# A fused adaLN and FFN kernel on one core: the conv's products moved in TensorE's row order, and the order of VectorE's and ScalarE's work around them

## The reference

```
h   = gelu(gelu(cond @ W0 + b0) @ W1 + b1);  att = softmax(h @ W2 + b2)
y   = einsum('boi,bih->boh', einsum('bk,koi->boi', att, weight), x) + (att @ bias_k)[:, :, None]
x   = x + y @ (A @ B.T).T + bias                       # rank 128
c   = conv1d(x, w, 9 taps, pad 4, 4 groups of 16 channels) + (cond @ cw.T + fside)[:, :, None]
g   = one_hot(argmax(c @ gate.T + expert_bias))        # 4 experts
out = x + c @ W_up + sum_e g_e * (c @ loraA_e.T) @ loraB_e.T
```

## Time and profile before

| | us |
|---|---|
| median of 3 executions | 1209.54 (1209.33 to 1210.42) |
| profiled execution | 1208.7 |
| its span | 1207.0 |
| TensorE busy | 1162.7 (96%) |
| weight loads busy | 1051.9 |
| VectorE busy | 751.2 (62%) |
| ScalarE busy | 503.1 (42%) |

### The profile page before, as it was taken

The page is one execution under the profiler, slowest core; times in us unless marked ns, Lnnn a source line. Parts: engine busy times, 40 slices in busy tenths (PEclk is TensorE's granted clock), DMA queues, the critical chain, the costliest instruction groups (busy, mean ns, idle before and its releaser), DMA issues.

```text
span 1207.0 us, 19065 instructions
## 1 busy us (share of the span) xinstructions
PE 1162.7 (96%) x7404; PEld 1051.9 (87%) x7404; DVE 751.2 (62%) x1440; ACT 503.1 (42%) x1048; POOL 4.0 (0%) x17
## 2 busy tenths in 40 slices
PE   6598999999999999999999999999999999999998
PEld 5487889889988989988989998988998898998898
DVE  6755766566666556666556666656666656666642
ACT  6544444334344334344334444433444433434320
POOL 1000000000000000000000000000000000000000
PEclk9699999999999999999999999999999999999999
DMA  9744545445544554544544544445544454454211
GB/s 339 240 92 94 141 104 140 113 138 136 118 102 129 132 126 131 141 97 115 143 113 132 140 110 105 137 112 139 137 112 106 130 129 128 132 126 109 56 50 53
DMA packets 115742, 151.78 MB, mean 126 GB/s; under 512 B 21324, under 2 KB 93516, under 8 KB 111404
## 3 DMA queue, kind: packets, MB, share of 16 engines
q1 hardware_dynamic: 115044, 148.36, 47.3%
q10 hardware_dynamic: 608, 2.20, 0.5%
HBM read 80.87 MB, written 35.68 MB: 97 GB/s over the span
## 4 chain that ended last, share of the span: by engine, by line
PE 88%; ACT 6%; DVE 3%; issue 2%; DMA 1%; SPq 0%; ACTq 0%
PE O L864 55%; PE F L847 9%; PE F L811 7%; ACT F L382 5%; PE F L835 4%; PE F L781 3%; PE F L782 3%; PE F L783 3%; PE O L882 2%; PE O L875 1%; PE F L798 1%; PE F L799 1%; SPq L228 0%; DMA xTr<-in_xT_dram 0%; DVE wks L642 0%
## 5 line engine op out<-in xcount | busy, mean ns | idle before, releaser
L864 PE MATMUL O<-Wh,yh 128*128 128x292 f32 (+2 forms) x1536 | 509.0, 331 | 3.2 <-DVE yl L576 3.2
L864 PE MATMUL O<-Wl,yh 128*128 128x292 f32 (+2 forms) x1536 | 498.6, 325 | 0.0
L864 PE MATMUL O<-Wh,yl 128*128 128x292 f32 (+2 forms) x1536 | 498.3, 324 | 0.0
L864 PEld LDWEIGHTS O<-Wh,yh 128*128 128x128 f32 x1536 | 290.6, 189 | 28.6 <-DVE yl L576 3.5
L864 PEld LDWEIGHTS O<-Wh,yl 128*128 128x128 f32 x1536 | 290.0, 189 | 22.5
L864 PEld LDWEIGHTS O<-Wl,yh 128*128 128x128 f32 x1536 | 290.8, 189 | 17.1
L382 ACT ACTIVATE F<-F,cbX 128x128 f32<-128x128 f32 x496 | 138.1, 341 | 219.0 <-PE F L835 218.9
L609 DVE TENSOR_TENSOR osb<-O,x 128x256 f32<-128x256 f32 (+1 forms) x192 | 97.7, 509 | 108.1 <-PE O L882 107.8
L568 DVE STREAM_TRANSPOSE yr<-F 128x512 f32<-128x512 f32 x128 | 91.4, 715 | 83.4 <-PE F L847 83.4
L309 ACT ACTIVATE u<-F 128x256 f32<-128x256 f32 x64 | 24.6, 385 | 263.4 <-PE F L783 219.0
L542 DVE TENSOR_TENSOR x<-F,x 128x512 f32<-128x512 f32 x128 | 87.6, 689 | 32.3 <-PE F L811 32.3
(11 more groups left out here) (126 smaller groups left out, 1470.3 us busy)
## 6 DMA issues: line engine op xcount, KB each, us to landing
x<-in_xP_dram SPq DMA_DIRECT2D x64, 516.0 KB, 4.4
Xr<-x SPq DMA_DIRECT2D x512, 64.5 KB, 2.5
xTr<-in_xT_dram SPq DMA_DIRECT2D x32, 1024.0 KB, 5.1
out_dram<-osb SPq DMA_DIRECT2D x64, 512.0 KB, 2.9
agb<-agb_scratch SPq DMA_DIRECT2D x31, 128.0 KB, 3.3
Wr<-in_Wd_dram SPq DMA_DIRECT2D x2, 1024.0 KB, 15.1
agg_scratch<-stage ACTq DMA_DIRECT2D x1, 2048.0 KB, 11.3
agg<-agg_scratch SPq DMA_DIRECT2D x60, 32.0 KB, 2.3
```

Source lines behind the costliest of these rows:

```text
L864: last = pe.matmul(O[c][:, 0:w_], w[:, t % YR, k, :], m[:, k, c0:c0 + w_], start=k == 0 and n_ == 0, stop=k == 7 and n_ == 2)
```

## The change

Three things are reordered; no instruction is added, removed or resized. On TensorE the shared products and their users stand at other rows. In VectorE's loop, one transposition of the conv and the expert chain of the second tile change places with their neighbours. In ScalarE's loop, zst of the second tile is copied ahead of the high parts of the next conv input. In the setup, ScalarE copies the first shared products ahead of vh of set 1 and of part 4 of the weights, and VectorE's list follows.

```diff
@@ scalar, setup
             xs(0, 0)
-            vhi(1)
-            w(4)
             pc(0, 0)
             pc(0, 1)
             xs(0, 1)
             ys(0, 0)
+            vhi(1)
+            w(4)
             w(5)
@@ scalar, loop, it > 0
                     pc(it + 1, 2)
                     ys(it + 1, 0)
                     pc(it + 1, 3)
+                    zt(2 * it + 1)
                     xs(it + 2, 0)
                     ys(it + 1, 1)
-                    zt(2 * it + 1)
                     bias(it + 3)
@@ vector, setup
             vv(1)
-            vlo(1)
             xd(0, 1)
             ty(0, 0)
             ty(0, 1)
-            w(4)
             ys(0, 0)
             xs(0, 1)
+            vlo(1)
+            w(4)
@@ vector, loop, it > 0
                     ty(it + 1, 0)
-                    ty(it + 1, 1)
                     txl(it + 3, 1)
                     f(t, 2)
+                    ty(it + 1, 1)
                     xd(it + 2, 0)
                     ys(it + 1, 0)
                     ty(it + 1, 2)
+                    zc(t + 1)
                     ty(it + 1, 3)
-                    zc(t + 1)
                     xs(it + 2, 0)
                     ys(it + 1, 1)
                     f(t + 1, 0)
@@ tensor, loop
-                    pp, cc = ((24, 27, 39, 42), (26, 29, 41, 44)) if it == 0 else ((16, 19, 22, 26), (19, 22, 26, 30))
+                    pp, cc = ((24, 28, 39, 42), (28, 32, 42, 45)) if it == 0 else ((16, 21, 26, 31), (21, 26, 31, 34))
                     if n in cc:
                         unit_c(it + 1, cc.index(n))
                     if n in pp:
```

## The result

The changed kernel takes 1190.76 us (median of 4, 1189.13 to 1191.15) against 1209.56 before (median of 4, 1209.33 to 1210.42): ratio 0.9841, 95% interval 0.9824 to 0.9858, or 18.8 us faster. The prediction was 1184.9 with a range of 1181 to 1192. The time lies in the range near its upper end, with 5.9 us less gain than forecast. The profiled execution took 1190.71, its span 1189.0.

What follows compares the result with a forecast made beforehand. TensorE's work (busy 96%) plus the places where it stands was taken to bound the kernel. 23.8 - 1.5 + 1.0 + 0.2 + 1.1 = 24.6 us off gave 1184.1 profiled, 1184.9 as median; range 1181 to 1192.

Steps and rivals of the forecast that it cites:

- part 1: Loop: shared products and users five rows apart remove two waits of 0.41 in each of 29 passes, 23.8 us off.
- wait at the pass's start: First weight load waits for VectorE's residual addition: 0.05 a pass, 1.5 us back; rival of 0.2 to 0.8, chance 0.18.
- The expert chain: VectorE, second tile: moved chain ends 1.6 ahead of TensorE's turn, costing nothing; behind the fourth transposition it would hold TensorE 1.1.
- SP's queue: Loop: raw-set loads issue 5.4 later, the next expert chain slips 0.4, its transposition has 2.1 of slack; no cost.
- the slower rival: Loop: late raw sets, with loads issuing slower, hold VectorE at Xd ahead of the expert chain; about 1228, chance 0.04.
- Pass 0: Later users lengthen the wait for expert values at row 36 to about 3.3; pass 0 together 0.2 us off.
- the case that I gave 0.22: Rival: the longer gap ahead of row 36 of pass 0 drops the clock, 1.7 more, 1186.6 us; chance 0.22.
- Setup: ScalarE's copies first: first users go at 48.3 instead of 49.28, row 0 at 54.4; 1.0 us off.
- Pass 1: Rows 20 and 21 (0.71) run inside the wait for ScalarE's copies, a second wait (0.41) goes: 1.1 us off.
- the fall of the clock near 108: Pass 0: clock drop behind the 2.63 gap costs 1.7 us; might vanish with the gap's new start, taken at nothing.

Runs made afterwards that it cites:

- a3: The changed kernel with ScalarE's loop order of before, zst of the second tile again behind the high parts of the next conv input: 1184.3 us.
- b2: The changed kernel with the first residual addition of the second tile ahead of yl in VectorE's loop: 1190.1 us.
- a4: The changed kernel with the rows of pass 0 put back to those of before: 1188.4 us.
- d1: The changed kernel with ScalarE's loop order and the rows of pass 0 both those of before: 1185.0 us.
- b1: The changed kernel with VectorE's expert chain of the first tile ahead of Xd of the last set in pass 30: 1190.1 us.
- c1: The changed kernel with zst back, the expert chain first in pass 0, and the expert chain ahead of Xd in pass 30: 1184.6 us.
- d2: Against d1, shared products and users in the loop four rows apart instead of five: 1187.2 us.
- b4: The changed kernel with VectorE's expert chain of the second tile back behind the fourth transposition: 1229.1 us.
- b3: The changed kernel with the expert chain behind VectorE's first transposition in pass 0 and zst copied ahead of Xh there: 1191.2 us.

## Why the prediction was right and where it was short

The time lies in the range, and its main term, part 1, is right in mechanism and size. But that the range holds it is partly luck: its upper part, up to 1192, was there for a wait at the pass's start of 0.3 in each pass, and that wait came out at 0.1. What filled it were the end, which the forecast had at nothing, and the clock in pass 0.

- **Part 1, right.** Both waits of each pass are gone, 58 in all; a pass without any other wait takes 35.02 (a3) where it was 35.84: 0.82, as worked out. That a wait of 0.35 costs 0.41 is confirmed by it. The spare of 0.4 was there (0.44).
- **The expert chain, right, a little off in size.** It ends 1.2 ahead of the transposition (forecast 1.6), and behind the fourth transposition it would cost 1.28 (forecast 1.1).
- **The new wait at the pass's start, right, undersized:** 0.10 against 0.05; a3 and b2 both remove it. The term that was too small is the way from VectorE's addition to TensorE's load, 0.12 and not 0.05; the chain up to the addition's end came out as worked out, 5.65 behind the load of the transposition (forecast 5.63).
- **SP's queue: the step that failed.** "So this costs nothing" had 2.1 of slack at the transposition, less the 0.4 by which the chain slips. That holds in passes with layer-0 work: 1.5 to 1.6 is left in most passes whose loads take 5.05, and there Xd was 7.07 behind the first of the eight loads, as forecast. It doesn't hold in pass 30, where TensorE comes to the transposition 3.5 sooner: 2.7 us at the end, of which a3 gives back all. And once the eight loads took 6.57, 0.4 us. The mechanism was in the text as the slower rival, priced with the slack of a full pass for all passes; I had not asked which pass has the least. The rival's "in the loop they take 5.0 to 5.1 throughout" was wrong too. The trace of before already has 12 of 56 sets of eight loads between 135 and 1135 us above 5.3, among them this one:

```profile
176.59 6.37 SPq L228 DMA_DIRECT2D Xr<-x  x8
```

- **Pass 0, the wait right, its price wrong.** The wait for the expert values grew to 3.7 at the loads (3.3 at the matmul), as forecast. The clock then fell, which I had taken at nothing with a bound of 1.7:

```profile
92.00:94.00 2.00, 0.00 (x0) 0.00 (x0) 1.76 (x10) 1.61 (x2) 0.00 (x0) 0.71 0.08 33
94.00:96.00 2.00, 1.96 (x6) 1.58 (x6) 1.80 (x2) 0.27 (x1) 0.00 (x0) 0.50 0.00 0
98.00:100.00 2.00, 2.00 (x10) 1.81 (x9) 0.69 (x1) 0.35 (x2) 0.00 (x0) 0.59 0.69 94
```

  These are stretches of the changed kernel, with the granted clock behind POOL, in the view of the earlier trace rows: 1.2 GHz from 92.8 to 99.6, of which TensorE ran from 94.0 on, so at most half of 5.6, 2.8 us. In a3, with the same orders up to there and the same wait, the clock stayed at the upper level, and pass 0 took 37.62 instead of 40.07:

```profile
92.00:94.00 2.00, 0.21 (x2) 0.21 (x3) 1.76 (x10) 1.61 (x2) 0.00 (x0) 1.00 0.05 21
94.00:96.00 2.00, 2.00 (x11) 1.65 (x11) 1.83 (x3) 0.27 (x1) 0.00 (x0) 1.00 0.00 0
```

  So the case that I gave 0.22 happened in this execution, at 2.5 us.
- **Setup, the size off.** 0.57 between shared product and users, not 1.0, since the shared products run at the lower clock too. That yl waited for VectorE's Wl was no term: the 6.1 from first users to row 0 didn't change. The stretch's 1.0 is not this term: most of it came from the sooner rise of the clock.
- **Pass 1, 1.2 against 1.1, but not shown.** With these rows in the loop pass 1 took 37.4 to 39.8 over the kernels, so agreement to 0.1 in one execution is luck.
- **The sum:** of the 6.6 us missing, the late raw sets and the wait at the pass's start, both behind zst's place, make some 4, and the clock in pass 0 makes 2.5.

What stays open is the price of pass 0's rows. a4 has it at 2.4 us, d1 against a3 at nothing. Passes 0 and 1 together took 75.2 to 79.2 over the kernels, with the same rows 76.1 to 79.2. In pass 1 the first copies start at 125.1 to 127.7 in all thirteen traces, 12.6 to 13.9 behind the raw set's first load, whether or not the clock fell near 108. This suggests that the raw set, and not TensorE, sets the first copies of pass 1, and that the fall of the clock near 108, for which I had 1.7 either way, is hidden. But it comes back: in the four traces without that fall (b1, c1, d1, d2) TensorE waited 2.1 to 3.1 for these copies, the clock fell there instead, for 3.4 us from 126.8 to 128.3 on, and pass 1 took 38.8 to 39.8; with the fall near 108 and the changed rows it took 37.4 to 39.2. That was only read from the traces.

## What to carry to other kernels

When a wait is hidden by moving work later, follow the chain that hangs on the moved work to the end of the pass, and then look for the pass with the least other work ahead of the place that waits: the cover there is what counts. Of edits made together each should be tried alone, since here one of three, zst's place, cost nearly a quarter of what the others gained. And a copy that waits for the bottleneck engine should not stand in a queue ahead of copies that could run meanwhile, unless its own user would else wait.

## What the runs showed of the hardware that was not expected

- The clock falls and rises at other places in executions of the same code. In pass 0, behind the same wait of 3.7 us, the granted clock was 0.50 for some 7 us after the changed order (92.8 to 99.6), in b2 and in b4, for about 3 in b1 (0.54 and 0.61 in the two stretches of 2 us from 94 on), and stayed at 1.00 in a3. Pass 0 took 40.0 to 40.1, 38.8 and 37.6. In pass 30 the clock fell for 3.4 us behind a wait of 2.4 (b3) and of 3.0 (b2), and not behind 2.9 (after), 2.7 (a4) and 3.1 (b4). The Trainium skill, TensorE: Matmul & The Clock Gate, section "What's actually happening", says that how much work runs at the lower clock varies from run to run, since the monitor runs free of the program; the traces agree, with these numbers.
- Eight loads in a row took 5.0 to 5.1 us to issue in most passes, but more than 5.3, up to 6.6, in 18 of the 57 sets of eight between 135 and 1135 us after (12 of 56 before), so a chain through SP varies by more than 1 us from pass to pass.
- A weight load needed its semaphore one matmul slot before the matmul's turn, so cover for a wait is to be counted to the load: 0.12 less with 256 columns. In d2 the copies ended at 514.58, 0.10 ahead of the matmul's turn, and the load was still 0.07 late.
